# Attention scores in three pieces with a PSUM bank each, instead of four units on three banks

## The reference

```python
q = (x @ Wq.T).reshape(B, S, G, rep, D)      # G=4 groups, rep=4 heads each, D=16
k = (x @ Wk.T).reshape(B, S, G, D)
v = (x @ Wv.T).reshape(B, S, G, D)
scores = einsum('bqgrd,bkgd->bgrqk', q, k) * scale + bias   # bias: -inf above the diagonal
attn = softmax(scores, axis=-1)
x = layernorm(x + einsum('bgrqk,bkgd->bqgrd', attn, v).reshape(B, S, Hd) @ Wo.T)
x = layernorm(x + ffn(x))    # 32 routed experts, 6 of them per token, and a shared expert
```

## Time and profile before

| | |
|---|---|
| median of 3 runs | 565.51 us (562.99 to 566.81) |
| the profiled execution | 565.8 us |
| its span, first to last instruction | 564.0 us |
| busy: TensorE matmul, VectorE, ScalarE, POOL | 459.8, 378.2, 321.9, 226.4 us |
| granted TensorE clock, mean | 0.942 of full |

### The profile page before, as it was taken

One profiled execution on the slowest core, in us unless ns is written; L12 is line 12 of the kernel. 1 busy time (PEld: TensorE's weight loads), 2 busy tenths in 40 slices (PEclk: granted clock), 3 DMA queues, 4 the chain that ended last, 5 costly groups with the idle time before them and its releaser, 6 DMA issues.

```text
span 564.0 us, 12967 instructions
## 1 busy us (share of the span) xinstructions
PE 459.8 (82%) x3190; PEld 377.7 (67%) x3191; DVE 378.2 (67%) x1745; ACT 321.9 (57%) x1093; POOL 226.4 (40%) x244
## 2 busy tenths in 40 slices
PE   4366779797968787767997999999999999992972
PEld 3254557575756555534556999898989898991761
DVE  4036385969697878974636677776767777772696
ACT  1059698878888979814102555555555555552133
POOL 0000000070716253477550657656566666563000
PEclk9669898889999989989999999999999999997897
DMA  4569659896978833289953555545455555523992
GB/s 130 125 221 269 153 139 267 228 273 164 242 170 234 203 103 102 77 307 416 416 198 82 168 153 166 160 145 168 139 154 158 156 160 158 143 63 121 420 409 95
DMA packets 67996, 107.92 MB, mean 191 GB/s; under 512 B 9189, under 2 KB 55018, under 8 KB 66416
## 3 DMA queue, kind: packets, MB, share of 16 engines
q1 hardware_dynamic: 54016, 75.15, 46.5%
q0 software_dynamic: 10752, 26.13, 14.0%
q10 hardware_dynamic: 3184, 6.13, 2.9%
HBM read 64.03 MB, written 43.33 MB: 190 GB/s over the span
## 4 chain that ended last, share of the span: by engine, by line
PE 55%; DVE 19%; DMA 10%; ACT 8%; issue 5%; SPq 2%; DVEq 0%; POOLq 0%; ACTq 0%; POOL 0%
PE bank L698 21%; PE bank L707 11%; DVE s_neg L980 5%; PE bank L688 5%; PE bank L637 5%; ACT probs L800 5%; DMA k_scratch<-k_lo 3%; PE bank L478 3%; DMA k_pack<-k_scratch 3%; PE bank L646 2%; PE bank L541 2%; ACT pT L811 2%; DMA xt<-xT 1%; DMA x1T_all<-x1T 1%; DVE ey_all L1339 1%
## 5 line engine op out<-in xcount | busy, mean ns | idle before, releaser
L1383 POOL DMA_INDIRECT routed<-rows,position x96 | 93.5, 974 | 194.5 <-DVE position L1144 166.9
L1393 POOL DMA_INDIRECT expert_out<-ey_all,out_row x128 | 130.1, 1017 | 93.4 <-issue 64.0
L800 ACT ACTIVATE probs<-s_neg,m_neg 128x128 f32<-128x128 f32 (+1 forms) x256 | 114.1, 450 | 38.1 <-DVE m_neg L980 37.9
L980 DVE CUSTOM_DVE_ANT_0 s_neg<-bank,bias_sb 128x128 f32<-128x128 f32 (+1 forms) x256 | 79.6, 351 | 54.7 <-PE bank L510 53.5
L898 ACT ACTIVATE eg<-bank 128x128 f32<-128x128 f32 x128 | 35.6, 278 | 88.9 <-PE bank L698 88.3
L707 PE MATMUL bank<-expert_w,ea 128*128 x256 | 78.8, 390 | 1.7 <-DVE ea L1296 0.6
L698 PEld LDWEIGHTS bank<-xgT,xn 128*128 128x128 f32 x512 | 66.5, 191 | 9.2 <-issue 5.6
L698 PE MATMUL bank<-xgT,xn 128*128 128x128 f32 x512 | 68.1, 276 | 3.6 <-issue 3.0
L510 PE MATMUL bank<-k_pack,q_pack 128*128 128x256 f32 (+1 forms) x128 | 58.3, 464 | 15.2 <-DMA k_pack<-k_scratch 12.6
L905 ACT ACTIVATE ey_all<-bank,pick 128x256 f32<-128x256 f32 x128 | 60.0, 469 | 1.8 <-DVE out_row L1309 1.5
L811 ACT ACTIVATE pT<-bank 128x512 f32<-128x512 f32 x96 | 55.8, 583 | 0.0
(11 more groups left out here) (160 smaller groups left out, 812.2 us busy)
## 6 DMA issues: line engine op xcount, KB each, us to landing
xg<-routed SPq DMA_DIRECT2D x128, 137.5 KB, 2.1
expert_w<-expert_out SPq DMA_DIRECT2D x16, 768.0 KB, 14.4
expert_w<-expert_weights SPq DMA_DIRECT2D x9, 1024.0 KB, 17.7
q_pack<-q_scratch SPq DMA_DIRECT2D x32, 256.0 KB, 5.0
routed<-empty SPq DMA_DIRECT2D x8, 550.0 KB, 12.8
k_pack<-k_scratch SPq DMA_DIRECT2D x16, 256.0 KB, 7.1
expert_w<-expert_weights ACTq DMA_DIRECT2D x3, 1024.0 KB, 13.5
xt<-xT SPq DMA_DIRECT2D x9, 256.0 KB, 7.8
```

Of the source, the lines that this page charges most:

```text
L800: act.activation(probs[g % 2][qb][:, 2 * pair + r, :], s_neg[u][:, r, 0:n], ACT.Exp, bias=m_neg[:, u, r:r + 1], scale=-1.0, accum_out=row_ ...
L980: dve.tensor_tensor_reduce(out=s_neg[u][:, r, 0:n], in0=SCORES[u][:, n * r:n * r + n], in1=bias_sb[:, REP * g + 2 * pair + r, SEQ - n:SEQ] ...
L1383: pool.indirect_dma_start(routed, bass.IndirectOffsetOnAxis(ap=position[b % ROW_BUFS][:, t, j:j + 1], axis=0), rows[b % ROW_BUFS][:, t, :] ...
L1393: pool.indirect_dma_start(expert_out, bass.IndirectOffsetOnAxis(ap=out_row[:, k:k + 1], axis=0), ey[k], None, bounds_check=TOKENS * TOPK - ...
```

## The change

The four units of a group are renumbered: units 0 and 1 are the first query block of the two pairs, units 2 and 3 the second block. The scores of units 0 and 1 become one piece: two 256-column matmuls into the two halves of bank 0. Unit 2 is a piece in bank 1 and unit 3 one in bank 2. TensorE issues a piece ahead of each of the three turns, where it issued a unit ahead of each turn and one behind the last. The first turn now holds the first query block of all four heads, the second and third the second query block with the first and the second key block; ScalarE's copies of the first two turns write four strips of 128 columns. A piece waits for the bias ops that read its bank a whole group earlier. The bias op of unit 0 waits for both matmuls of its piece, and every unit's bias op waits for the exps that read its s_neg buffer a group earlier, where unit 0's alone did.

```diff
-        SCORES = [S_BANK[0], S_BANK[1], S_BANK[2], S_BANK[1]]
+        SCORES = [S_BANK[0][:, 0:SEQ], S_BANK[0][:, SEQ:2 * SEQ], S_BANK[1], S_BANK[2]]
...
-            def scores(b, par, h, g, u):
-                pair, qb = u // 2, u % 2
-                unit = 16 * b + 4 * g + u
-                if g == 0 and u == 0:
-                    pe.wait_ge(qk_packed[par], 96 * (h + 1))
-                need(pe, biased, 2 * (unit - (4 if u % 2 == 0 else 2)) + 2)
-                n = (qb + 1) * P
-                pe.matmul(SCORES[u][:, 0:2 * n], q_pack[par][:, 2 * g + pair, P * qb:P * qb + P],
-                          k_pack[par][:, g, :, 0:n], start=True, stop=True).then_inc(scores_ready, 1)
+            def scores(b, par, h, g, part):
+                first = 16 * b + 4 * g
+                if part == 0:
+                    if g == 0:
+                        pe.wait_ge(qk_packed[par], 96 * (h + 1))
+                    need(pe, biased, 2 * (first - 3) + 2)
+                    for pair in range(2):
+                        pe.matmul(SCORES[pair], q_pack[par][:, 2 * g + pair, 0:P], k_pack[par][:, g, :, 0:P],
+                                  start=True, stop=True).then_inc(scores_ready, 1)
+                else:
+                    pair = part - 1
+                    need(pe, biased, 2 * (first + 2 + pair - 4) + 2)
+                    pe.matmul(SCORES[2 + pair][:], q_pack[par][:, 2 * g + pair, P:2 * P], k_pack[par][:, g, :, :],
+                              start=True, stop=True).then_inc(scores_ready, 1)
...
-                if j < 2:
-                    for r in (2 * j, 2 * j + 1):
-                        for qb in range(2):
-                            at = SEQ * (r % 2) + P * qb
-                            last = pe.transpose(pb[:, at:at + P], probs[g % 2][qb][:, r, 0:P], ident)
-                else:
-                    for r in range(REP):
-                        last = pe.transpose(pb[:, P * r:P * r + P], probs[g % 2][1][:, r, P:2 * P], ident)
+                for r in range(REP):
+                    src = probs[g % 2][0][:, r, :] if j == 0 else probs[g % 2][1][:, r, P * (j - 1):P * j]
+                    last = pe.transpose(pb[:, P * r:P * r + P], src, ident)
...
-                        if g < GROUPS - 1:
-                            scores(b, par, h, g + 1, u)
-                        elif ahead:
-                            scores(b + 1, o, h + par, 0, u)
                         if u < 3:
+                            if g < GROUPS - 1:
+                                scores(b, par, h, g + 1, u)
+                            elif ahead:
+                                scores(b + 1, o, h + par, 0, u)
                             turn_probs(b, g, u)
...
-                pair, qb = u // 2, u % 2
+                pair, qb = u % 2, u // 2
...
-                dst = pT0[g][:, 2 * j:2 * j + 2, :] if j < 2 else pT1[g][:]
-                act.activation(dst.rearrange("p r t -> p (r t)"), T_BANK[(3 * g + j) % 2][:], ACT.Copy
+                dst = pT0[g][:, :, P * j:P * j + P] if j < 2 else pT1[g][:]
+                act.activation(dst, T_BANK[(3 * g + j) % 2][:].rearrange("p (r t) -> p r t", r=REP), ACT.Copy
...
+                need(dve, probs_ready, 2 * (unit - 4) + 2)
                 if u == 0:
-                    need(dve, probs_ready, 2 * (unit - 4) + 2)
...
-                need_apart(dve, scores_ready, unit + 1, passed)
+                need_apart(dve, scores_ready, unit + (2 if u == 0 else 1), passed)
```

More of the change, by code:

```diff
@@ L620, in _ @@
             project_kv(0, 0, True, True)
-            for u in range(4):
-                scores(0, 0, 0, 0, u)
+            for part in range(3):
+                scores(0, 0, 0, 0, part)
             pe.wait_ge(cst_loaded, 16)
```

## The result

The changed kernel takes 568.53 us (median of 12 runs, 567.79 to 572.23) where the kernel before takes 565.36 beside it (12 runs, 562.99 to 567.72): a ratio of 1.0066, 95% interval 1.0042 to 1.0089. The forecast was 564.7, a small saving; the kernel is some 3 us slower. The profiled execution after took 568.15, with a span of 566.3.

The account below looks back on a forecast made before the run. The prediction took the ring of TensorE, VectorE and ScalarE in the attention loop as the bound, 25.9 us a batch. Savings of −0.10, −0.21, −0.41 and −0.12, about −0.8, gave 564.7 us on the median's scale, range 559.5 to 569.

Parts of the forecast that it names:

- The ring: Attention loop: 7.0 us of TensorE, 13.3 of VectorE, 5.6 of ScalarE in turn bound each batch, 25.9 us, unchanged.
- The waits and copies at nothing: VectorE's and ScalarE's stretches: bias ops' second waits and copies writing four strips were each taken to cost 0.
- The rival of the new waits: VectorE's gapless stretch: six more two-wait bias ops a batch at 0.10 each cost 3.6 us, giving 568.3; chance 0.07.
- The sum of −0.84: Attention loop: total of the path savings −0.10, −0.21, −0.41 and −0.12, taken as −0.8 us.
- theory C: Attention loop, from the follow-up runs, not the forecast: the changed loop itself is slower on the average.
- Term (c): Batches 6 and 7: 512 score moves ahead of the third turn, a 256 of 0.12 comes in: −0.41 and −0.12.
- Term (a): Batch 1, paced by ScalarE: group 2's second bias op becomes narrow, 0.23 for 0.33: −0.10.
- Term (b): Ahead of batch 3, TensorE at lower clock: 512 score of 0.43 moves ahead, a 256 of about 0.22 enters: −0.21.
- Behind the loop nothing is touched, and each stage there starts from the end of the one before, so the saving should arrive whole.: Stages after the attention loop: they pass on the loop's saving of about 0.8 us unchanged.
- The clock rival: Attention loop hand-overs: new order moves TensorE's clock, up to 559.2 (chance 0.13) or down to 566.8 (0.07).

Follow-up runs that it names:

- before_waits: Kernel before plus only the change's extra waits: every unit's first bias op waits for the exps of four units back, 93 more VectorE instructions; ratio 1.0078.
- before_pad93: Kernel before with 186 already met waits, 93 more instructions, in VectorE's program ahead of its second q split; ratio 1.0068.
- before_pad256: Kernel before with 512 already met waits, 256 more instructions, in two places early in VectorE's program; ratio 1.0068.

## Why the prediction was wrong

**The ring.** Right. TensorE 7.00, then group 2's first bias op behind the last score, ScalarE's wait for group 1's last unit gone and 0.66 before group 2 (the forecast said about 1; ScalarE now also stands 0.89 for the values' copy): 25.9 to 26.2 us a batch at full clock.

**The waits and copies at nothing.** Right where they stand: 0.08 of overlap, 584 ns, and at most 0.07 us a batch in before_waits. The rival of the new waits had 568.3, close to the 568.53 measured; that is luck, for its sign, bias ops that start behind their predecessor's end, did not appear. Wrong in what else an instruction does. Each extra wait is an instruction of its own on VectorE, and 93 of them moved the slot loop's code: 1.8 us, shown by before_pad93, which has 93 instructions elsewhere, and by before_waits, which has the waits and nothing else of the change.

**The sum of −0.84.** Too large by nearly all. From one batch's product with the reciprocals to the next batch's, comparing only stretches at full clock in the profiles of either order: 24.13 became 23.96 (batch 1 to 2), 25.91 became 25.95, 25.94 became 25.96, 24.12 became 24.00, 22.94 became 22.85, and the last 17.35 became 17.6, after:

```profile
220.64 0.44 PE L546 MATMUL bank<-cst,l_wide 128*128 128x128 f32 x2
...
238.26 0.44 PE L546 MATMUL bank<-cst,l_wide 128*128 128x128 f32 x2
```

That sums to −0.1 (one pair, from batch 3 to 4, was never at full clock in the old order); theory C falls with it. Term (c) was mis-sized: batches 6 and 7 gave 0.12 and 0.09 instead of 0.41 and 0.12, the first because its row was at the lower clock; and the end of the last batch took 0.25 back, where ScalarE waits for bias ops of its last two groups for 0.49, 0.32 and 0.57 (before: 0.30, 0.45, 0.35). Term (a) lies in the first pair, which gave 0.17 for the 0.10 forecast. Term (b) was read at the lower clock, and its pair (batch 2 to 3) gained nothing: +0.04 at full clock, and 27.4 us before and after in the two first profiles, each with 6.8 us at the lower one.

**"Behind the loop nothing is touched, and each stage there starts from the end of the one before, so the saving should arrive whole."** This is the step that failed. Nothing behind the loop is edited, yet the loss is there: 1.8 us in the slots through the code's place (shown, though not how the place does it); 2.8 us in the shared expert and 1.1 in the tail where TensorE restarts at the lower clock (shown where it happens; that the change is its cause is not).

**The clock rival** looked for the clock in the attention loop, at the hand-overs. In the page's row (before: the earlier trace rows) four of the loop's slices lost a tenth and one gained one, and behind it the 19th slice fell from 9 to 7 (the shared expert) and the 38th from 8 to 7 (the tail):

```profile
PEclk9669798888999898987999999999999999997797
```

## What to carry to other kernels

A wait that costs nothing where it stands is still an instruction: where a later rolled loop runs in step with another engine, count how far each engine's code moves, and try a few places before judging a change of half a percent. Here, whether TensorE paid 2.7 us behind an idle stretch of 3.45 went with a shift of one microsecond upstream; take such idle time away before weighing small gains ahead of it. And compare runs at equal granted clock: here that turned three overlapping ratios of 1.0068 into differences of 2.6, 2.1 and 0.5 us.

## What was not expected of the hardware

The slot loop has steady patterns with one, two or three of sixteen equal copies at 0.7 us and not 0.43, of 26.28 to 26.34 us a pass with one or two and some 26.55 with three, and a kernel keeps the one it falls into up to its last pass but one. On VectorE 140 instructions of met waits took 13.7 us (before_pad256's idle time ahead of the second q split), some 98 ns each. The kernel before has runs at a granted clock of 0.950 and more with spans of 557.4 to 560.4, 6 us and more under one of 566.4 at 0.928.
